# Summing two of four taps on TensorE in the causal convolution of layer 1

## The reference

```python
xc = conv_general_dilated(xs.transpose(0, 2, 1), conv_w, (1,), [(D_CONV - 1, 0)], feature_group_count=D_INNER)
xc = silu(xc + conv_b[None, :, None]).transpose(0, 2, 1)
x_dbl = einsum('nld,ed->nle', xc, x_proj_w)
dt, Bm, Cm = split(x_dbl, [DT_RANK, DT_RANK + D_STATE], axis=-1)
delta = softplus(einsum('nlr,dr->nld', dt, dt_proj_w) + dt_proj_b)
```

## Time and profile before

| | us |
|---|---|
| median of three runs | 28573.06 (28565.04 to 28573.14) |
| the profiled execution | 28574.97 |
| its span | 28573.2 |
| first GpSimd copy of the stage to its last multiplication | 8144 to 9068 |
| VectorE busy in 8600 to 8800 | 197.67 of 200 |
| ScalarE busy there | 156.23 of 200 |
| TensorE busy there, at a mean clock of 0.65 | 130.37 of 200 |
| GpSimd busy there | 116.25 of 200 |

### The profile page before, as it was taken

How to read it: one execution, slowest core, us unless ns; L and a number is a source line. 1 busy time by engine, 2 the same in 40 slices (tenths; PEclk the granted TensorE clock), 3 DMA queues, 4 the chain that set the end, 5 groups by cost and what they waited for, 6 DMA issues and landing times. The chain is left out here.

```text
span 28573.2 us, 328305 instructions
## 1 busy us (share of the span) xinstructions
PE 23019.3 (81%) x97488; PEld 6738.0 (24%) x97488; DVE 25438.8 (89%) x16283; ACT 14602.9 (51%) x20067; POOL 22850.1 (80%) x10240
## 2 busy tenths in 40 slices
PE   8878888888566888888887888888865888888885
PEld 3322222222232222222233222222212322222222
DVE  3489999999579999999976999999996899999996
ACT  1255555555266555555514655555542655555552
POOL 0169999999036999999971799999980499999992
PEclk9878888888666888888868888888877788888887
DMA  2241222211554222221266322221226622222225
GB/s 86 96 139 42 49 49 49 49 41 40 196 186 162 45 49 49 49 46 42 49 236 216 112 48 49 49 49 42 45 86 225 202 48 49 49 49 43 44 49 184
DMA packets 1151553, 2417.75 MB, mean 85 GB/s; under 512 B 99990, under 2 KB 638578, under 8 KB 1139948
## 3 DMA queue, kind: packets, MB, share of 16 engines
q1 hardware_dynamic: 1147956, 2393.61, 30.4%
q10 hardware_dynamic: 1728, 1.70, 0.0%
HBM read 1371.87 MB, written 1023.05 MB: 84 GB/s over the span
## 5 line engine op out<-in xcount | busy, mean ns | idle before, releaser
L1589 POOL TENSOR_TENSOR scan_hc<-scan_bc,scan_h 128x1024 f32<-128x1024 f32 x6912 | 16107.7, 2371 | 115.4 <-DVE scan_h L1766 114.2
L1766 DVE TENSOR_TENSOR_SCAN scan_h<-scan_da,scan_state,scan_dbu 128x1024 f32<-128x1024 f32 x6912 | 15989.4, 2338 | 143.6 <-ACT scan_da L1643 137.3
L1680 PE MATMUL scan_da<-scan_dd,scan_ssel 32*128 32x512 f32 x27648 | 9115.4, 746 | 3001.5 <-DVE scan_h L1766 2768.2
L1643 ACT ACTIVATE scan_da<-scan_da,scan_a_cur 128x1024 f32<-128x1024 f32 x6912 | 7516.3, 1087 | 7738.0 <-PE scan_da L1680 7730.6
L1680 PE MATMUL scan_p_du<-scan_dd,scan_ssel 32*128 32x512 f32 x27648 | 9216.5, 746 | 457.3 <-DVE scan_dbu L1753 176.2
L1753 DVE TENSOR_TENSOR scan_dbu<-scan_p_du,scan_bc 128x1024 f32<-128x1024 f32 x4608 | 5562.5, 1207 | 386.5 <-PE scan_p_du L1680 349.4
L1575 POOL TENSOR_TENSOR scan_dbu<-scan_bc,scan_dus 128x1024 f32<-128x1024 f32 x2304 | 5466.0, 2372 | 59.9 <-ACT scan_dus L1617 58.2
L1680 PEld LDWEIGHTS scan_da<-scan_dd,scan_ssel 32*128 32x128 f32 x27648 | 2456.2, 217 | 10295.7 <-DVE scan_h L1766 8715.7
L1697 PE MATMUL scan_p_y<-scan_hc,scan_rsel 128*32 128x512 f32 x27648 | 4784.3, 773 | 14.9 <-POOL scan_hc L1589 14.4
L1680 PEld LDWEIGHTS scan_p_du<-scan_dd,scan_ssel 32*128 32x128 f32 x27648 | 2415.2, 211 | 3536.0 <-DVE scan_dbu L1753 2961.9
L1622 ACT ACTIVATE scan_state<-scan_h,scan_a_cur 128x1 f32<-128x1 f32 x6912 | 2024.1, 293 | 1580.4 <-DVE scan_h L1766 1471.6
(11 more groups left out here) (211 smaller groups left out, 13639.4 us busy)
## 6 DMA issues: line engine op xcount, KB each, us to landing
scan_bc<-bc_d SPq DMA_DIRECT2D x576, 512.0 KB, 12.0
du_d<-prep_useq SPq DMA_DIRECT2D x384, 576.0 KB, 3.7
delta_d<-prep_delta SPq DMA_DIRECT2D x384, 576.0 KB, 4.8
y_d<-scan_y SPq DMA_DIRECT2D x576, 384.0 KB, 5.2
merge_y<-y_d SPq DMA_DIRECT2D x384, 576.0 KB, 5.5
scan_dd<-delta_d SPq DMA_DIRECT2D x1136, 192.0 KB, 4.8
scan_dd<-du_d SPq DMA_DIRECT2D x1136, 192.0 KB, 6.5
xs_d<-proj_xs_o SPq DMA_DIRECT2D x96, 588.0 KB, 3.3
```

Of the source, the lines that this page charges most:

```text
L1589: nc.gpsimd.tensor_tensor(hc[:, u % HC_SLOTS, :], c, h[:, u % H_SLOTS, :], ALU.mult).then_inc(hc_ready, 1)
L1643: nc.scalar.activation(da[u % DELTA_BANKS][:], da[u % DELTA_BANKS][:], ACT.Exp, scale=a_cur[:, slot(u)[0], u % UNITS:u % UNITS + 1]).then_ ...
L1680: return nc.tensor.matmul(dst[:, half * H:(half + 1) * H], ssel[rows, i, :], dd[rows, s, m, j, :], start=True, stop=True)
L1766: nc.vector.tensor_tensor_scan(h[:, v % H_SLOTS, :], da[v % DELTA_BANKS][:], dbu[:, v % DBU_SLOTS, :], state[:, v % UNITS:v % UNITS + 1], ...
```

## The change

TensorE sums taps 2 and 3 of each half tile with two matmuls against a diagonal matrix, into a bank `p_tap`; `p_dbl` gives up its second bank for it. ScalarE takes the sum out with the bias into `useq`, a half at a time, in place of reading `raw`. VectorE adds two taps, not three. The places of the steps change as well: tile 2 of pair i+3 is now begun one turn later than before, ahead of `take`, tiles 0 and 1 of pair i+4 stand ahead of SiLU. GpSimd waits for TensorE's sums before it overwrites `raw`. One more weight, `diag`, is loaded.

```diff
-        MULTS = SEQ_TAPS - 1
+        MULTS = SEQ_TAPS - 2
-        p_dbl = [ph.ps(f"p_dbl{b}", [P, 512]) for b in range(PAIR)]
+        diag = ph.sb("diag", [P, SEQ_TAPS - MULTS, 2, P])
+        p_dbl = ph.ps("p_dbl", [P, 512])
+        p_tap = ph.ps("p_tap", [P, 512])
...
+                        sp.dma_start(diag[:], w["tapd"]).then_inc(loaded, 16)
...
-                    g.wait_ge(first_ready, max((j - 1) * TILES + m + 1, 0) + ONE)
+                    g.wait_ge(summed, max((j - 1) * TILES + m + 1, 0) * PAIR + ONE)
...
-                    t.wait_ge(dtv_ready, max(v - 1, 0) + ONE)
+                    t.wait_ge(dtv_ready, v + ONE)
...
+                def sum_taps(j, m):
+                    t.wait_ge(raw_ready, j * TILES + m + 1 + ONE)
+                    for b in range(PAIR):
+
+                        t.wait_ge(first_ready, (j * TILES + m) * PAIR + b + ONE)
+                        for n in range(SEQ_TAPS - MULTS):
+                            at = MULTS + n + b * N
+                            last = nc.tensor.matmul(p_tap[:, 0:N], diag[:, n, m // 2, :], raw[:, m, at:at + N], start=(n == 0),
+                                                    stop=(n == SEQ_TAPS - MULTS - 1))
+                        last.then_inc(summed, 1)
...
                 for i in range(-AHEAD, PAIRS):
                     for b in range(PAIR):
                         if pair(i + 1):
                             expand((i + 1) * PAIR + b)
+                    if pair(i + 3):
+                        sum_taps(i + 3, 2)
                     for b in range(PAIR):
                         if pair(i + 2):
                             project((i + 2) * PAIR + b)
+                    if pair(i + 4):
+                        for m in range(2):
+                            sum_taps(i + 4, m)
...
                 def first_tap(j, m):
-                    a.wait_ge(raw_ready, j * TILES + m + 1 + ONE)
 
                     a.wait_ge(du_stored[j % SLOTS], 16 * PAIR * (j // SLOTS) + ONE)
-                    nc.scalar.activation(useq[:, j % SLOTS, m, :], raw[:, m, HALO:HALO + DW], ACT.Identity, bias=conv_b[:, m:m + 1],
-                                         scale=tapv[:, m, SEQ_TAPS - 1:SEQ_TAPS]).then_inc(first_ready, 1)
+                    for b in range(PAIR):
+                        a.wait_ge(summed, (j * TILES + m) * PAIR + b + 1 + ONE)
+                        nc.scalar.activation(useq[:, j % SLOTS, m, b * N:(b + 1) * N], p_tap[:, 0:N], ACT.Identity,
+                                             bias=conv_b[:, m:m + 1]).then_inc(first_ready, 1)
...
-                    if pair(i + 4):
-                        first_tap(i + 4, 0)
+                    if pair(i + 3):
+                        first_tap(i + 3, 2)
                     if pair(i + 2):
                         for b in range(PAIR):
                             take((i + 2) * PAIR + b)
+                    if pair(i + 4):
+                        for m in range(2):
+                            first_tap(i + 4, m)
                     if pair(i + 3):
                         silu(i + 3)
-                    if pair(i + 4):
-                        for m in range(1, TILES):
-                            first_tap(i + 4, m)
```

More of the change, by code:

```diff
@@ L1175, in prepare_causal @@
         raw_ready = ph.sem("raw_ready")
+        summed = ph.sem("summed")
         first_ready = ph.sem("first_ready")
@@ L1303, in project @@
                     t.wait_ge(useq_ready, v // PAIR + 1 + ONE)
-                    t.wait_ge(dtv_ready, max(v - 1, 0) + ONE)
+                    t.wait_ge(dtv_ready, v + ONE)
                     for m in range(TILES):
-                        last = nc.tensor.matmul(p_dbl[v % 2][:, 0:N], wx[:, m, :], piece(v)[:, m, :], start=(m == 0), stop=(m == 2))
+                        last = nc.tensor.matmul(p_dbl[:, 0:N], wx[:, m, :], piece(v)[:, m, :], start=(m == 0), stop=(m == 2))
                     last.then_inc(dbl_done, 1)
@@ L1318, in expand @@
                     last.then_inc(dt_done, 1)
-                t.wait_ge(loaded, 16 * 6 + ONE)
+                def sum_taps(j, m):
[7 more added lines that the diff above has]
+                        last.then_inc(summed, 1)
+                t.wait_ge(loaded, 16 * 7 + ONE)
                 for i in range(-AHEAD, PAIRS):
@@ L1347, in take @@
                     a.wait_ge(bc_stored[v % DTV_SLOTS], 16 * (v // DTV_SLOTS) + ONE)
-                    nc.scalar.activation(dtv[:, v % DTV_SLOTS, :], p_dbl[v % 2][:, 0:N], ACT.Identity, bias=ones[:]).then_inc(dtv_ready, 1)
-                a.wait_ge(loaded, 16 * 6 + ONE)
+                    nc.scalar.activation(dtv[:, v % DTV_SLOTS, :], p_dbl[:, 0:N], ACT.Identity, bias=ones[:]).then_inc(dtv_ready, 1)
+                a.wait_ge(loaded, 16 * 7 + ONE)
                 for i in range(-AHEAD, PAIRS):
@@ L1373, in add_taps @@
                     own = useq[:, j % SLOTS, m, :]
-                    d.wait_ge(first_ready, j * TILES + m + 1 + ONE)
+                    d.wait_ge(first_ready, (j * TILES + m + 1) * PAIR + ONE)
                     for tap in range(MULTS):
@@ L1392, in softplus @@
                     nc.vector.tensor_tensor(delta[:, v % DELTA_SLOTS], p_dt[v % 2][:, :, 0:N], sp_b[:, v % PAIR], ALU.max).then_inc(delta_ready, 1)
-                d.wait_ge(loaded, 16 * 6 + ONE)
+                d.wait_ge(loaded, 16 * 7 + ONE)
                 for i in range(-AHEAD, PAIRS):
@@ L2570, in layouts @@
         w["l1_tapv"] = per_tile(g["conv_w"].reshape(HID, SEQ_TAPS))
+        w["l1_tapd"] = diagonals(g["conv_w"].reshape(HID, SEQ_TAPS)[:, 2:])
         w["l1_conv_b"] = per_tile(g["conv_b"])
```

## The result

The changed kernel takes 29014.85 us (median of 4 runs, 29010.69 to 29044.47); the kernel before, beside it, 28569.05 (28561.48 to 28573.14). The ratio is 1.0159 [1.0147, 1.0172]: 446 us slower. The forecast was 29044. Four single executions among all kernels here, at 30362 to 46527 us and a lower granted clock, belong to a slower state of the chip: the ratios leave them out, and without them no median moves by more than 4.2 us. The profiled execution of after took 29010.69 us, span 29007.8.

The account below looks back on a forecast made before the run. VectorE was taken to bound the kernel before, a ScalarE-TensorE chain after: 45 turns of 28.8 us (+437), start +24, end about +10, so 28575 + 471 = 29046, 29044 as median; range 28900 to 29340.

Parts of the forecast that it names:

- T: TensorE's sum of a half tile, two matmuls: 1.48 us at full clock, 2.77 at half; five a turn on the chain.
- ScalarE's own 13.99 us: ScalarE's work in one turn: Exp, Ln, SiLU, three table loads and six takes of 0.564 us, 13.99 us together.
- the hand-overs: Passing between ScalarE and TensorE on the chain, 0.10 and 0.04 us, five of each: 0.70 us a turn.
- P: TensorE's `project` of a piece, three matmuls: 2.14 us at full clock, 4.05 at half; two a turn on the chain.
- The clock: TensorE's clock falls 4.3 us into idleness, rises 5.2 us after a cold start; adds 1.29 us for T, 1.17 for P.
- The sum: Whole stage: 45 turns of 28.8 us give +437, the start +24, the end about +10, together +471 us.
- VectorE at 11.3 to 19.6 a turn, hidden: VectorE's work a turn with six additions at 1.02 to 2.4 us, under the 28.8 us turn.
- Each a cost of nothing: Work of VectorE, GpSimd, SyncE's stores and the `diag` load costs nothing while the chain is longer than 20 us.
- ScalarE's 5.2 us to spare: In the kernel before, ScalarE is busy some 14.4 of 19.55 us a turn and has 5.2 us to spare.
- Warm throughout: Rival, 20%: TensorE's clock rises at the first T or never falls; turns of 26.4 us, 28930 us in total.
- Faster: Rival, 3%: TensorE and ScalarE run ahead, VectorE saves three additions; turns of 16.5 to 14.4 us, about 28390 in total.
- Cold throughout: Rival, cold or mostly cold 20%: the exchange's gaps keep TensorE's clock down; turns of 36.6 us, 29410 in total.

Follow-up runs that it names:

- the kernel that keeps the clock up: The changed kernel with nine more full-size matmuls a turn, written to the free `p_dbl` in TensorE's gap; 28924.22 us, ratio 1.0124 to the kernel before.
- the spread kernel: The changed kernel with both banks used in turn by all sums and projects, and ScalarE's takes placed between its long instructions; 28508.44 us, ratio 0.998.
- the kernel with the spread order and single banks: The order of the spread kernel, but one bank for the sums and one for the projects, as in the changed kernel; 29116.48 us, ratio 1.0192.
- The kernel with four extra matmuls: The kernel with the spread order and single banks, plus four matmuls a turn into the free `p_dbl` ahead of tile 1's second half; 28840.19 us, ratio 1.0095.

## Why the prediction was right

The mechanism is as told, and shown from both sides: halving T shortens the program, relieving VectorE does nothing, using the banks in turn takes back half. By the prediction's steps:

- **ScalarE's own 13.99 us and the hand-overs.** Exp and Ln take 2.22 a pair where 2.33 and 2.31 were put. One of them costs what it did (1155 ns in the mean); the two of a pair overlap a little, as Ln did in the kernel before, and doubling the mean put 0.2 us a turn too much. The hand-overs: TensorE's gaps of 0.73 to 0.76 less the take's 0.58 leave 0.15 to 0.18 a round trip, 0.14 predicted.
- **T and P.** At full clock T is 1.45 to 1.56 (1.48 predicted) and P 2.17 (2.14). At half clock T is 2.93 (2.77).
- **The clock.** Idleness begins at about 8725.1 (8723.57 + 1.56) and the clock falls at about 8728.9, 3.8 us later; predicted 4.3. It is back at about 8735.7, 3.2 us behind the start of the cold T, where 5.2 was predicted. In this turn P hardly loses (2.36); in the next two it takes 3.80 and 2.84, and turns of 27.8, 29.3 and 28.3 us follow each other in rotation. The sum put 1.17 us on P in every turn; it lost 0.2, 1.6 and 0.7.
- **The sum.** First cut 8183.24 to the cut of pair 45 at 9462.10: 28.42 a turn, 28.8 predicted; +418 for +437. From the first raw copy (8131.78) to the first cut 51.5 us, 26.4 before: +25 for +24, which is partly luck: six T ran at half clock and not four (some 3 us more), but the 3.4 us put down for SiLU and its table load lay beside a T. Behind pair 45, 49.2 to the last multiplication's end where it was 36.8: +12 for +10. So the stage is 456 us longer, 471 predicted. The profiled executions differ by 436 only: the rest of the program was about 20 us shorter, 12.6 of it ahead of the stage (its first copy begins at 8131.78, at 8144.42 before). That is of the size of the runs' own spread, and is not attributed.
- **VectorE at 11.3 to 19.6 a turn, hidden.** Each addition takes 1.03 us (mean 1.48 before), the low end. VectorE's idle time was put at 10 us a turn and is 17: it is busy 11.4 of 28.4. "Each a cost of nothing" held in after.
- **Two prices without a term of their own.** Each alone, in the kernel before, ScalarE's new places cost 84 us and the second `p_dbl` bank 109. In after the first is covered, as far as ScalarE's waits show (none is for VectorE). The second is not: the second P stands on the chain and makes a part of the 218.3 us of waits for `p_dbl`. The prediction had them on the chain but didn't say what giving up that bank costs by itself, and the expectation of that run took ScalarE's 5.2 us to spare as enough.
- **The rivals.** *Warm throughout* was put at 28930; the kernel that keeps the clock up measures 28924, so the sum was right and the condition absent. *Faster* needed TensorE to run ahead; the spread kernel does, and gets turns of 16.8 where that rival had 16.5 at the upper end. It comes to 28508 and not to 28390: its 45 steady turns are 17.4 us on average, and the turn before was 19.1 over the stage and not the 19.55 of the earlier trace rows. *Cold throughout* didn't happen in after in the steady turns, but its mechanism exists: the kernel with the spread order and single banks had it for most of its turn of 31 us.

What the Trainium skill says in "TensorE: Matmul & The Clock Gate", section "What's actually happening", that sustained busyness releases the clock and idleness brings it back, agrees with the steady turns of after (0.50 to 1.00 at 8735.7, during P; 1.00 to 0.50 at 8728.9, in the gap). It was near to misleading all the same: in the kernel with the spread order and single banks TensorE is busy 477 of 600 us at a mean clock of 0.66, and the exchange itself ran at half. So the doubt behind the cold rival was real.

The Trainium skill's rule in "SBUF — State Buffer", section "Who interferes with whom", that a VectorE instruction with two SBUF inputs and a GpSimd one that reads SBUF contend, agrees too: with six additions and GpSimd idle beside most of them the mean falls from 1481 to 1026 ns. Only nobody waited for it.

## What to carry to other kernels

A PSUM bank that one engine fills and an in-order engine empties makes the two work in series. Add up the fills that the consumer will stand and wait for, and hold that against its spare time, here 12.8 us a turn against 5.2, before counting what another engine saves. To keep such an offload, share the banks in turn among all tensors that pass this way, and put each take beside a long instruction of the consumer: the two together turned +1.6% into -0.2%. A relief for the bounding engine pays only if the new chain is shorter than the turn which that engine set before: 28.4 us against 19.1 in the change, 17.4 in the spread kernel.

## What was not expected of the hardware

An exchange with holes of 0.73 to 0.76 us ran at either clock. At the stage's start in after six T ran at 2.93 us before one ran at 1.53 (the rise lies between these two lines):

```profile
8151.90 2.93 PE L1332 MATMUL prep_p_tap<-prep_raw,prep_diag 128*128 128x384 f32 x4 [0.73 <-ACT prep_useq L1357]
8155.59 1.53 PE L1332 MATMUL prep_p_tap<-prep_raw,prep_diag 128*128 128x384 f32 x4 [0.76 <-ACT prep_useq L1357]
```

That is 22 us of exchange at half clock (8133.56 to 8155.59), while in the steady turn above the clock was up 3.2 us behind the start of the cold T, with a P following without a hole. The kernel with four extra matmuls shows both cases with one and the same sequence of work: turns with every T at 1.56 us or less stand beside turns with T of 2.93. Matmuls with no use gained time in three kernels: 91 us in after (nine a turn), 276 in the spread order with single banks (four a turn) and 41 in the kernel before with one `p_dbl` bank (nine a turn).
